# Two banks of query products issued in turns, and the last third of an output issued in turns with the bank of keys

## What is computed

```
x = x + layer0(x)      # LN, q = xn@Wq (16 heads of 64), k,v = xn@Wkv, softmax(q k' / 8 + bias), @Wo, LN
x = x + layer1(x)      # the same, with q and k of each head divided by their norms, scores times 8,
                       # and a bias by relative position
```

## Time and profile before

| | us |
|---|---|
| median of 3 runs (2564.84 to 2567.8) | 2565.9 |
| the profiled execution | 2567.3 |
| its span, first to last instruction | 2565.4 |
| TensorE products busy, in the span | 2464.6 (96%) |
| VectorE busy | 1684.0 (66%) |
| ScalarE busy | 1630.1 (64%) |
| GpSimd busy | 903.8 (35%) |
| mean granted TensorE clock | 0.984 |

### The profile page before, as it was taken

One profiled execution on the slowest core, in us unless ns is written; L12 is line 12 of the kernel. 1 busy time (PEld: TensorE's weight loads), 2 busy tenths in 40 slices (PEclk: granted clock), 3 DMA queues, 4 the chain that ended last, 5 costly groups with the idle time before them and its releaser, 6 DMA issues.

```text
span 2565.4 us, 49723 instructions
## 1 busy us (share of the span) xinstructions
PE 2464.6 (96%) x14753; PEld 2150.2 (84%) x14753; DVE 1684.0 (66%) x4817; ACT 1630.1 (64%) x6621; POOL 903.8 (35%) x1691
## 2 busy tenths in 40 slices
PE   1599999999999999999999999999999999999997
PEld 1488888888888888888888888888888888888885
DVE  5566676666666666666666666667666666666664
ACT  2466666666666666666666666666666666666664
POOL 1433343333333433433333334334333343343341
PEclk7799999999999999999999999999999999999998
DMA  6110110110111011010010011010011001001000
GB/s 198 29 32 23 35 31 22 35 35 24 29 35 30 23 35 31 23 35 31 23 35 31 23 35 31 23 35 31 22 35 35 26 27 35 31 23 35 31 19 22
DMA packets 85974, 85.92 MB, mean 33 GB/s; under 512 B 46624, under 2 KB 48704, under 8 KB 85952
## 3 DMA queue, kind: packets, MB, share of 16 engines
q1 hardware_dynamic: 81264, 83.65, 10.9%
q10 hardware_dynamic: 4688, 2.01, 0.4%
HBM read 48.89 MB, written 16.79 MB: 26 GB/s over the span
## 4 chain that ended last, share of the span: by engine, by line
PE 95%; DVE 1%; ACT 1%; issue 0%; POOL 0%; POOLq 0%; DVEq 0%
PE psum L328 32%; PE psum L401 29%; PE psum L358 12%; PE psum L387 10%; PE psum L367 5%; PE psum L345 5%; PE psum L315 2%; PE psum L336 1%; ACT probs L490 0%; DVE probs L601 0%; DVE x_lo L549 0%; DVE neg_max L607 0%; ACT x_hi L449 0%; DVE bn_out L625 0%; DVE bn_in L537 0%
## 5 line engine op out<-in xcount | busy, mean ns | idle before, releaser
L490 ACT ACTIVATE probs<-probs,neg_max 128x129 f32<-128x129 f32 (+3 forms) x2048 | 716.2, 353 | 461.4 <-DVE neg_max L607 461.4
L705 POOL TENSOR_TENSOR weights<-probs,den_inv 128x256 f32<-128x256 f32 (+3 forms) x1024 | 437.3, 453 | 1562.2 <-DVE den_inv L613 1562.1
L692 POOL TENSOR_TENSOR masked_bias<-bias,pad_neg 128x516 f32<-128x516 f32 (+3 forms) x512 | 419.1, 853 | 18.2 <-POOL pad_neg L688 9.2
L358 PEld LDWEIGHTS psum<-keys,q_t 128*128 128x128 f32 x2048 | 324.8, 188 | 75.0 <-issue 49.4
L490 ACT ACTIVATION_READ_ACCUMULATOR probs<-probs,neg_max 128x1 f32 x2048 | 386.0, 188 | 0.0
L601 DVE TENSOR_TENSOR probs<-psum,masked_bias 128x388 f32<-128x388 f32 (+1 forms) x512 | 232.8, 491 | 232.5 <-PE psum L358 225.3
L358 PE MATMUL psum<-keys,q_t 128*128 128x258 f32 (+3 forms) x2048 | 351.0, 313 | 0.3 <-ACT q_t L481 0.3
L328 PE MATMUL psum<-w_hi,x_hi 128*128 128x384 f32 x1536 | 342.7, 345 | 6.3 <-DVE x_lo L549 6.3
L328 PE MATMUL psum<-w_lo,x_hi 128*128 128x384 f32 x1536 | 330.6, 337 | 0.0
L328 PE MATMUL psum<-w_hi,x_lo 128*128 128x384 f32 x1536 | 330.4, 337 | 0.0
L328 PEld LDWEIGHTS psum<-w_hi,x_hi 128*128 128x128 f32 x1536 | 267.9, 190 | 13.4 <-DVE x_lo L549 7.7
(11 more groups left out here) (111 smaller groups left out, 3251.8 us busy)
## 6 DMA issues: line engine op xcount, KB each, us to landing
xa<-in_x_dram SPq DMA_DIRECT2D x64, 256.0 KB, 2.7
x_res<-in_x_dram SPq DMA_DIRECT2D x64, 256.0 KB, 2.6
x_res<-x SPq DMA_DIRECT2D x64, 256.0 KB, 2.3
out_dram<-x_out SPq DMA_DIRECT2D x64, 256.0 KB, 2.1
raw<-in_L_cond_Wq_dram SPq DMA_DIRECT2D x8, 512.0 KB, 7.6
raw<-in_L_cond_Wo_dram SPq DMA_DIRECT2D x8, 256.0 KB, 5.8
raw<-in_L_cond_Wout_dram SPq DMA_DIRECT2D x8, 256.0 KB, 7.3
v_part<-v_diff SPq DMA_DIRECT2D x128, 8.0 KB, 1.7
```

The source lines that it names most:

```text
L358: m = nc.tensor.matmul(block(SP[g % 2], b, GROUP_AT[g % 2]), q_t[:, g // 2, b, :], keys[u.layer][:, :, 0:WIDTH[b]], start=True, stop=True)
L490: x_ = nc.scalar.activation(s, s, ACT.Exp, bias=neg_max[:, g, k, e:e + 1], accum_out=den[:, g, k, e:e + 1])
L692: m = nc.gpsimd.tensor_tensor(block(masked_bias[u.layer], b), block(bias[u.layer], b), pad_neg[u.layer][:, 0:WIDTH[b]].unsqueeze(1).unsque ...
L705: m = nc.gpsimd.tensor_tensor(places[b], block(probs[:, g // 2, :], b)[:, :, 1:1 + n], den_inv[:, g, k, :].unsqueeze(2).to_broadcast([P, 2 ...
```

## The change

In TensorE's program, project now handles one bank and yields after each product, so that two such streams can be zipped. project_queries issues banks 0 and 1 in turns (bank 0's first). project_out's body becomes output_part, which yields after each product, and output_and_keys issues output part 2 and bank 2 in turns until the eight output products are out, and then the last four of bank 2; it stands in early slots alone. In late and meet the keys come as before, and then the queries in turns. The order of the other stages and the orders of the other engines are unchanged, and so is every semaphore, each raised by the last product of its bank.

```diff
-            def project(u, banks):
-                for b in banks:
-                    if b == 2:
-                        wait(pe, x_lo_done, u.done)
-                    else:
-                        wait(pe, qt_copied[b], u.prev)
...
+            def project(u, b):
+                if b == 2:
+                    wait(pe, x_lo_done, u.done)
+                else:
+                    wait(pe, qt_copied[b], u.prev)
+                lo, hi = QB[b]
+                n = 0
+                for xs, ws in ((x_hi, w_hi), (x_hi, w_lo), (x_lo, w_hi)):
+                    for c in range(KC):
+                        m = nc.tensor.matmul(Q[b][:, 0:hi - lo], xs[:, c * P:(c + 1) * P], ws[u.layer][:, c, lo:hi],
+                                             start=(n == 0), stop=(n == 3 * KC - 1))
+                        n += 1
+                        if n == 3 * KC:
+                            m.then_inc(proj_done[b], 1)
+                        yield
+
+            def project_queries(u):
+                for _ in zip_longest(project(u, 0), project(u, 1)):
+                    pass
+
+            def project_keys(u):
+                for _ in project(u, 2):
+                    pass
...
-            def project_out(u, p):
+            def output_part(u, p):
...
-                if p == 2:
-                    m.then_inc(y_done, 1)
+                    if p == 2 and j == PAIRS - 1:
+                        m.then_inc(y_done, 1)
+                    yield
+
+            def project_out(u, p):
+                for _ in output_part(u, p):
+                    pass
+
+            def output_and_keys(v, w):
+                steps = zip_longest(output_part(v, 2) if v else (), project(w, 2))
+                for _ in steps:
+                    pass
...
             def early(u, v, w, n):
                 opening(u, v, w)
-                run_stages((part(project_out, 2), v), (part(project, (2,)), w), (part(transpose_p, (0, 1)), u),
-                           (part(project, (0, 1)), w), (part(transpose_p, (2, 3)), u))
+                output_and_keys(v, w)
+                run_stages((part(transpose_p, (0, 1)), u), (project_queries, w), (part(transpose_p, (2, 3)), u))
                 closing(u, w)
 
             def late(u, v, w, n):
                 opening(u, v, w)
-                run_stages((part(project, (2, 0, 1)), w), (part(transpose_p, (0, 1)), u),
+                run_stages((project_keys, w), (project_queries, w), (part(transpose_p, (0, 1)), u),
                            (part(project_out, 2), v), (part(transpose_p, (2, 3)), u))
                 closing(u, w)
 
             def meet(u, v, w, n):
...
-                           (part(project, (2, 0, 1)), w), (part(transpose_p, (0, 1, 2, 3)), u))
+                           (project_keys, w), (project_queries, w), (part(transpose_p, (0, 1, 2, 3)), u))
                 closing(u, w)
```

More of the change, by code:

```diff
@@ L1 @@
 from contextlib import ExitStack
+from itertools import zip_longest
 import concourse.bass as bass
```

## The result

The change made the kernel slower: 2658.2 us (median of four runs, 2655.1 to 2661.1) against 2566.2 (four runs, 2564.8 to 2567.8), a ratio of 1.036, 95% interval 1.034 to 1.037. The profiled execution took 2660.4 us around a span of 2658.6. That is 92 us more; 80 were forecast, with 2646 us as the time and 2585 to 2670 as the range.

A forecast was written before the change was run, and what follows sets the result against it. TensorE's list of products was taken to bound the kernel. Stalls of 38.4 us in late slots, 39.1 in early slots and 2.8 at the ends sum to +80.3, giving 2646 us, range 2585 to 2670.

The forecast's parts named there:

- A product's price: On TensorE, a 384-column product stays at 0.174 us in turns; gain and cost of alternating banks taken as 0.
- Rivals 1 and 2: TensorE: alternation makes products cheaper; 1, stalls stay, 2578 us at full bound, chance 0.14; 2, stalls partly covered, 2542, chance 0.08.
- Rival 3: Both slots: signals move but nobody waits longer, no change, 2566 us; chance 0.03.
- The late slot's wait: Before TensorE's query transposes in late slots: bank 0's late signal delays ScalarE and VectorE's last scaling, 0.62 us lost.
- The early slot's wait: Before TensorE's query transposes in early slots: ScalarE's second query copy can start 0.63 us later, all of it lost.
- What the pair held before: Two steady slots before the change: TensorE busy 38.03 of 38.12 us, nothing else late by more than 0.1 us a slot.
- Part 2 is free: Output and keys in turns, early slots: y complete 1.22 us later, price 0 because TensorE's 24 query products hide it.
- loses nearly all its slack: ScalarE's o_hi for the next output, late slot: VectorE's work moves 0.75 us, 0.13 more than TensorE.
- rival 4: TensorE's clock: idling 0.6 us every slot may lose the granted 1.00, queries alone costing 450 us in all; chance 0.02.

The follow-up runs named there:

- the run with the copy ahead of the root: The change with ScalarE's early order turned, bank 1's copy ahead of the root for the next input: 2652.2 us.
- the three orders above: Kernel before, first three query transposes ahead of bank 1's wait, copied-weights waits last before the values, late o_hi ahead of the output's root: 2538.9 us.
- its own run: Output and keys in turns alone, query banks one after the other as in the kernel before: 2564.7 us, ratio 0.9996.
- the transposes, o_hi: Kernel before with first three query transposes ahead of bank 1's wait: 2562.9 us; kernel before with late o_hi ahead of the output's root: 2559.7 us.
- the transposes ahead: First three query transposes moved ahead of the wait for bank 1: 2649.7 us on the change, 2562.9 us on the kernel before.
- the change with three orders: The change plus query transposes ahead of bank 1's wait, copied-weights waits last before the values, late o_hi ahead of the output's root: 2587.3 us.

## Why the prediction was right, and what it missed

**A product's price.** Right. In turns it is 0.173 us for 384 columns and 0.41 for one of each kind. The seams between banks had pointed that way, but thinly: a seam holds one change of bank, and 14 ns are little in rows rounded to 10. The runs with products in turns are what shows it. Rivals 1 and 2 fall with this: there was nothing to weigh against the stalls. Rival 3, that nobody waits longer, falls by the waits. The 14 ns above one column a cycle remain, and it wasn't tried what they are. The Trainium skill's formula for an isolated product (TensorE: Matmul & The Clock Gate, Back-to-back issue gap) gives 162.5 ns for 384 columns, an estimate from the page; the streams of products here stay at 173 ns, in turns or not.

**The late slot's wait.** Right: 0.62 forecast; the queries' start to the query transposes grew from 7.24 to 7.87 us, 0.63. The steps came where they were put, within 0.03 us: roots, copies and scaling in the order of ScalarE's queue, and the last scaling 0.78 us late (it ended 2.78 us after the first transpose of weights, and now ends 3.56 after it), where 0.75 was put. (The prediction's own times give 1321.79 - 1321.18 = 0.61, not 0.62.)

**The early slot's wait.** Right: 0.63 forecast, 5.07 to 5.69 us from the queries' start to the query transposes, 0.62. But "all of it is lost" at the copy of bank 1 was half the story, as the run with the copy ahead of the root showed: the values' wait for the copies of weights holds nearly the same time behind it.

**What the pair held before.** Misread, with no harm to the sum. The prediction took from 38.03 us of busy time in 38.12 that nothing else is late by more than 0.1 us a slot. The starts show 0.17 in the early slot and 0.13 and 0.03 in the late one, which the overlapping records hide; the three orders above took them away. The earlier trace rows has 232 products and 231 loads, too, since its window cuts through them; equal in number they are in the whole program, 14,753 each.

**Part 2 is free.** Right, shown by its own run: y's statistics moved from 1332.99 (2.16 us after the third output part began) to 1341.77 (3.36 after), 1.20 us, and no reader on TensorE waited.

**The step that was mis-sized** is the sentence that o_hi "loses nearly all its slack". I had put a cost of 0 to it; it measured 0.28 us a pair. o_hi started 1.48 us before the output in both traces (1323.96 and 1325.44, 1331.53 and 1333.01), behind the root, and the root behind VectorE. ScalarE before, and after the change:

```profile
1323.53 0.29 ACT L437 ACTIVATE ln_out<-mv_out,eps_col 128x1 f32<-128x1 f32 x1 [0.17 <-DVE mv_out L627]
1323.96 1.25 ACT L503 ACTIVATE o_hi<-psum,null_v_col 128x512 fp32r<-128x512 f32 x2
...
1331.09 0.29 ACT L460 ACTIVATE ln_out<-mv_out,eps_col 128x1 f32<-128x1 f32 x1 [0.18 <-DVE mv_out L650]
1331.53 1.25 ACT L526 ACTIVATE o_hi<-psum,null_v_col 128x512 fp32r<-128x512 f32 x2
```

I had compared VectorE's 0.75 with TensorE's 0.62, a lag of 0.13. But TensorE's own delay at the end of the late slot was only 0.50, since the 0.13 us that it used to wait before the values (transposes to values 1.12, now 0.99) had vanished behind the larger wait. With VectorE's measured 0.78 the lag was 0.28, against a slack that was already used up (0.03 of wait stood there before). Net +0.15 a pair (0.16 by the pair's own 1.41, against 0.62 + 0.63), and 62 pairs make 10 of the 13 us between the 80.3 forecast and the 93.2 by which the span grew. The remaining 3 lie in the slots at the ends, where I had 2.8 us and the trace has 93.2 - 62 x 1.41 = 5.8. How much of them is waits and how much the granted clock there (0.94 in the last five slots, 0.97 before) stays open.

**The clock** stayed at 1.00 in spite of 0.5 us and more of idle time in every slot, so rival 4 fell, and with it stretches of 20 and 24 products that alternate banks ran at the full clock. The Trainium skill's warning about cycling through PSUM banks (the same page, A second HAM failure mode) did not come true here.

## What to carry to other kernels

When products of two results are issued in turns, both results come at the end: count how many products later the first one is complete, and follow its reader's queue to the point where the main engine comes back for it. Where that reader serves two results one after the other, staggering them is the pipelining. And a wait that is removed can leave the time as it was, because the next queue holds it: here two of them removed one at a time showed 0.2% each (the transposes, o_hi), all three together 1%.

## What the runs showed of the hardware

The order of waits on one engine has a price. The values start 0.44 to 0.50 us after the last copy that holds them when three other waits, long fulfilled, stand behind that one (in the kernel before's late slots, and in the runs with the transposes ahead or the copy ahead of the root), and 0.14 us after it when it is the last (the change with three orders). The trace shows such a time as "issue", in which TensorE waited for nothing.

The granted clock at the end of the program differed between traces of kernels that do the same work there. Eight output products of the last unit took 3.55 us at 0.50 in the kernel before (2552.93 to 2556.48) and 1.96 us at 1.00 in the run with the transposes ahead (2551.36 to 2553.32).
